# Moving the PSUM copies of tiles 1 to 14 from ScalarE to VectorE, and more single-row fetches to ScalarE and SyncE

## What is computed

```python
x0 = emb[ids].reshape(ids.shape[0], -1)
x = x0
for i in range(cross_w.shape[0]):            # 3 cross layers
    s = x @ cross_w[i]
    x = x0 * s[:, None] + cross_b[i] + x
h = relu(x0 @ w1 + b1)                       # 1664 -> 1024
h = relu(h @ w2 + b2)                        # 1024 -> 512
h = relu(h @ w3 + b3)                        # 512 -> 256
logit = concatenate([x, h], axis=1) @ out_w + out_b
return sigmoid(logit)
```

## Time and profile before

| | us |
|---|---|
| median of 3 runs (529.99 to 531.2) | 531.18 |
| the profiled execution | 530.56 |
| its span on the core | 528.8 |
| so outside the span | 1.76 |
| TensorE matmuls busy | 480.8 (91%) |
| VectorE busy | 186.4 (35%) |
| ScalarE busy (without issuing DMAs) | 84.7 (16%) |
| GpSimd busy | 379.6 (72%) |

### The profile page before, as it was taken

How to read it: one execution, slowest core, us unless ns; L and a number is a source line. 1 busy time by engine, 2 the same in 40 slices (tenths; PEclk the granted TensorE clock), 3 DMA queues, 4 the chain that set the end, 5 groups by cost and what they waited for, 6 DMA issues and landing times.

```text
span 528.8 us, 11324 instructions
## 1 busy us (share of the span) xinstructions
PE 480.8 (91%) x2912; PEld 442.2 (84%) x2912; DVE 186.4 (35%) x391; ACT 84.7 (16%) x159; POOL 379.6 (72%) x407
## 2 busy tenths in 40 slices
PE   2699899899999989899898989999899898999997
PEld 1399698898989889798887988888898888989996
DVE  5766414232142423224242321424232142423325
ACT  4642111111011111102011110101111010101111
POOL 5777776777777777777777777777777777777720
PEclk9999999999999999999999999999999999999999
DMA  7971111111111111111111111111111111111100
GB/s 234 387 263 29 28 29 27 28 29 27 29 29 29 28 28 30 29 29 29 27 29 26 30 27 30 26 30 29 26 30 25 30 27 28 27 28 28 28 10 2
DMA packets 19700, 24.90 MB, mean 47 GB/s; under 512 B 9305, under 2 KB 10292, under 8 KB 19636
## 3 DMA queue, kind: packets, MB, share of 16 engines
q0 software_dynamic: 12800, 13.13, 11.2%
q1 hardware_dynamic: 4770, 10.74, 5.7%
q10 hardware_dynamic: 2066, 0.31, 0.3%
HBM read 24.41 MB, written 0.01 MB: 46 GB/s over the span
## 4 chain that ended last, share of the span: by engine, by line
PE 55%; POOL 14%; issue 10%; ACTq 9%; DMA 5%; DVE 4%; ACT 3%; POOLq 0%; DVEq 0%
PE l_bank L717 41%; POOL x_raw L347 14%; ACTq L387 8%; DMA x_raw<-in_L_rec_emb,idx 4%; PE x_bank L717 4%; PE x_bank L729 4%; PE h_bank L771 3%; ACT xT_hi L400 2%; DVE x_raw L516 2%; ACTq L384 1%; PE l_bank L802 1%; DVE xT_lo L523 1%; PE h_bank L741 1%; DVE h2T_lo L528 1%; ACT h2T_hi L411 1%
## 5 line engine op out<-in xcount | busy, mean ns | idle before, releaser
L347 POOL DMA_INDIRECT x_raw<-in_L_rec_emb,idx x400 | 378.8, 947 | 125.5 <-issue 107.7
L717 PE MATMUL l_bank<-w_hi,xT_hi 128*128 128x342 f32 (+1 forms) x624 | 144.9, 333 | 3.5 <-DVE xT_lo L523 3.3
L717 PE MATMUL l_bank<-w_lo,xT_hi 128*128 128x342 f32 (+1 forms) x624 | 137.9, 321 | 0.0
L717 PE MATMUL l_bank<-w_hi,xT_lo 128*128 128x342 f32 (+1 forms) x624 | 137.7, 321 | 0.0
L717 PEld LDWEIGHTS l_bank<-w_hi,xT_hi 128*128 128x128 f32 x624 | 104.0, 191 | 7.9 <-DVE xT_lo L523 5.6
L717 PEld LDWEIGHTS l_bank<-w_lo,xT_hi 128*128 128x128 f32 x624 | 106.8, 191 | 0.0
L717 PEld LDWEIGHTS l_bank<-w_hi,xT_lo 128*128 128x128 f32 x624 | 106.3, 190 | 0.0
L523 DVE TENSOR_TENSOR xT_lo<-x_bank,xT_hi 128x512 fp32r<-128x512 f32 (+1 forms) x66 | 38.2, 578 | 158.5 <-ACT xT_hi L400 158.5
L400 ACT ACTIVATE xT_hi<-x_bank 128x512 fp32r<-128x512 f32 (+1 forms) x66 | 33.5, 507 | 270.3 <-PE x_bank L729 220.4
L729 PE MATMUL x_bank<-identity,x_raw 128*128 128x128 f32 x208 | 34.7, 279 | 27.0 <-DVE x_raw L516 27.0
L729 PEld LDWEIGHTS x_bank<-identity,x_raw 128*128 128x128 f32 x208 | 25.0, 142 | 36.7 <-issue 31.0
(11 more groups left out here) (94 smaller groups left out, 296.5 us busy)
## 6 DMA issues: line engine op xcount, KB each, us to landing
ids<-in_L_rec_emb SPq DMA_DIRECT2D x1152, 0.2 KB
ids<-in_L_rec_emb ACTq DMA_DIRECT2D x896, 0.2 KB
w_raw<-in_L_rec_w SPq DMA_DIRECT2D x18, 512.0 KB, 15.0
x_raw<-in_L_rec_emb,idx POOLq DMA_INDIRECT x400, 2.4
b_rows<-in_L_rec_b SPq DMA_DIRECT2D x1, 512.0 KB
b_rows<-in_L_rec_b SPq DMA_DIRECT2D x1, 256.0 KB
ids<-in_r_ids SPq DMA_DIRECT2D x1, 208.0 KB, 2.7
b_rows<-in_L_rec_b SPq DMA_DIRECT2D x1, 128.0 KB
```

The costliest lines, as they stand in the source:

```text
L347: pool.indirect_dma_start(out=dst, out_offset=None, in_=emb, in_offset=rows).then_inc(landed, 16)
L717: done = pe.matmul(bank[:, 0:b - a], x[:, k, :], w[:, k, a:b], start=(k == 0 and n == 0), stop=(k == last_k and n == 2))
```

## The change

1. The fields fetched row by row are those of chunk 10, the last chunk of group 2 (before: of chunk 12, in group 3). So the places are waited for by `make_whole` of group 2. SyncE fetches field 21 of tiles 2 to 14 (13 tiles, before 9). The rows of the biases, five DMAs, are issued by ScalarE in the first step, ahead of `x_hi(0, 1)`, and no longer by SyncE.
2. ScalarE fetches field 20 of ten tiles (3, 4, 5, 6, 8, 9, 10, 11, 13, 14; before seven tiles).
3. From tile 1 to 14 VectorE makes the copies `x_hi`, `h1_hi` and `h2_hi`, each right ahead of the subtraction that reads it.
4. ScalarE's step t is then: wait until group 0 of tile t is transposed, place what belongs to tile t, and fetch 104 rows in four shares of 26.
5. In tile 15 nothing is fetched row by row; ScalarE makes its copies there and in tile 0 as before.

`LAST_GROUPS` and the pacing of GpSimd stay. GpSimd now fetches chunk 12 of every tile and leaves out of chunk 10 what the others fetch: 393 gathers where it issued 400, that is 25 fields of tiles 2, 7 and 12, 24 of the other tiles from 3 to 14, and 26 of tiles 0, 1 and 15.

```diff
-    SP_TILES = [2, 4, 6, 8, 9, 10, 12, 14, 15]
+    SP_TILES = list(range(2, TILES - 1))
-    SP_FIELD = F - 2
+    SP_FIELD = GROUPS[2][-1] * FPK + 1
-    ACT_TILES = [3, 5, 7, 9, 11, 13, 15]
-    ACT_FIELD = F - 1
+    ACT_TILES = [3, 4, 5, 6, 8, 9, 10, 11, 13, 14]
+    ACT_FIELD = GROUPS[2][-1] * FPK
-    ACT_SHARES = [8, 12, 4, 16, 12, 12]
+    ACT_SHARES = [26, 26, 26, 26]
...
-            sync.wait_ge(idx_ready, 3)
-            for rows, vec in ((b1_rows, b1), (b2_rows, b2), (b3_rows, b3), (out_w_rows, out_w[D:D + N3, 0]), (out_b_rows, out_b)):
-                sync.dma_start(rows[:, :], vec.rearrange("(o n) -> o n", o=1).broadcast_to([P, rows.shape[1]])).then_inc(rows_loaded, 16)
...
             def fetch(share):
+                while share > 0 and fetched[0] < P * len(ACT_TILES):
+                    j, p = fetched[0] // P, fetched[0] % P
+                    if p == 0 and j >= ACT_BUFS:
+                        act.wait_ge(act_placed, j - ACT_BUFS + 1)
+                    row, rows = AT_ROWS.index((ACT_FIELD, ACT_TILES[j])), min(share, P - p)
+                    regs = [act.alloc_register(f"act_row{j}_{p + i}") for i in range(rows)]
+                    act.load(regs, at_bytes[row:row + 1, p:p + rows])
+                    for i, reg in enumerate(regs):
...
+                    fetched[0] += rows
+                    share -= rows
...
             def step(t):
-                fetch(ACT_SHARES[0])
-                x_hi(t, 0)
-                fetch(ACT_SHARES[1])
-                h2_hi(t - 1)
-                fetch(ACT_SHARES[2])
-                x_hi(t, 1)
-                fetch(ACT_SHARES[3])
-                x_hi(t, 2)
+                if t in SP_TILES or t in ACT_TILES:
+                    act.wait_ge(x_transposed, NG * t + 1)
                 if t in SP_TILES:
                     sp_place(t)
                 if t in ACT_TILES:
                     act_place(t)
-                fetch(ACT_SHARES[4])
-                x_hi(t, 3)
-                fetch(ACT_SHARES[5])
-                h1_hi(t)
+                for share in ACT_SHARES:
+                    fetch(share)
...
+            def x_hi(t, g):
+                dve.wait_ge(x_transposed, NG * t + g + 1)
+                ks = groups(t)[g]
+                dve.tensor_copy(xT_hi[:, ks[0]:ks[-1] + 1, :].rearrange("p k b -> p (k b)"),
+                                x_bank[g % 2][:, 0:len(ks) * P]).then_inc(xT_hi_ready, 1)
...
+            def step(t):
+                make_whole(t, 0)
+                x_hi(t, 0)
+                x_lo(t, 0)
+                l2_out(t - 1)
+                make_whole(t, 1)
+                x_hi(t, 1)
+                x_lo(t, 1)
+                h2_hi(t - 1)
+                h2_lo(t - 1)
+                for g in range(2, NG):
+                    make_whole(t, g)
+                    x_hi(t, g)
+                    x_lo(t, g)
+                l1_out(t)
+                dots_out(t)
+                h1_lo(t)
+                l3_out(t - 1)
```

More of the change, by code:

```diff
@@ L44, in dcn_ranker_kernel @@
     LOW_BITS = 2 ** (H.bit_length() - 1) - 1
-    SP_TILES = [2, 4, 6, 8, 9, 10, 12, 14, 15]
+    SP_TILES = list(range(2, TILES - 1))
     SP_REGS = 32
-    SP_FIELD = F - 2
+    SP_FIELD = GROUPS[2][-1] * FPK + 1
     SP_BUFS = 4
-    assert SP_FIELD // FPK in GROUPS[-1] and SP_FIELD // FPK in LAST_GROUPS[3]
-    ACT_TILES = [3, 5, 7, 9, 11, 13, 15]
-    ACT_FIELD = F - 1
+    ACT_TILES = [3, 4, 5, 6, 8, 9, 10, 11, 13, 14]
+    ACT_FIELD = GROUPS[2][-1] * FPK
     ACT_BUFS = 2
-    ACT_SHARES = [8, 12, 4, 16, 12, 12]
-    assert ACT_FIELD // FPK in GROUPS[-1] and all(
-        sum(ACT_SHARES) * (t - 1) >= P * (j + 1) for j, t in enumerate(ACT_TILES)) and P % sum(ACT_SHARES) == 0
+    ACT_SHARES = [26, 26, 26, 26]
+    assert all(sum(ACT_SHARES) * (t - 1) >= P * (j + 1) for j, t in enumerate(ACT_TILES))
+    ONE_RUNS = [(SP_FIELD, range(2, TILES - 1)), (ACT_FIELD, range(3, 7)), (ACT_FIELD, range(8, 12)), (ACT_FIELD, range(13, 15))]
+    AT_ROWS = [(f, t) for f, tiles in ONE_RUNS for t in tiles]
+    assert sorted(AT_ROWS) == sorted([(SP_FIELD, t) for t in SP_TILES] + [(ACT_FIELD, t) for t in ACT_TILES])
     ROW = E * 4
@@ L154, in dcn_ranker_kernel @@
         at_bytes = sb("at_bytes", [ONE_BY_ONE, P], I32)
-        at_row = {t: i for i, t in enumerate([t for t in SP_TILES if t % 2 == 0] + [t for t in SP_TILES if t % 2])}
         VR = (2 * CROSS + 1) * K1
@@ L291, in _ @@
                     regs = [sync.alloc_register(f"sp_row{i}_{p + j}") for j in range(SP_REGS)]
-                    sync.load(regs, at_bytes[at_row[t]:at_row[t] + 1, p:p + SP_REGS])
+                    row = AT_ROWS.index((SP_FIELD, t))
+                    sync.load(regs, at_bytes[row:row + 1, p:p + SP_REGS])
                     for j, reg in enumerate(regs):
@@ L367, in split_hi, with load_rows @@
                 act.activation(hi, raw, ACT.Copy).then_inc(hi_split, 1)
+            def load_rows():
+                act.wait_ge(idx_ready, 3)
+                for rows, vec in ((b1_rows, b1), (b2_rows, b2), (b3_rows, b3), (out_w_rows, out_w[D:D + N3, 0]), (out_b_rows, out_b)):
+                    act.dma_start(rows[:, :], vec.rearrange("(o n) -> o n", o=1).broadcast_to([P, rows.shape[1]])).then_inc(rows_loaded, 16)
             def sp_place(t):
@@ L377, in fetch @@
             def fetch(share):
[L379 to L389, removed]
+                while share > 0 and fetched[0] < P * len(ACT_TILES):
[6 more added lines that the diff above has]
+                    for i, reg in enumerate(regs):
+                        at = act.snap(reg, donate=True, min_val=0, max_val=(2 * H - 1) * ROW)
+                        act.dma_start(act_rows[j % ACT_BUFS][p + i:p + i + 1, :].bitcast(U8),
+                                      emb_bytes[:, bass.DynSlice(at, ROW)], bounds_check="skip_entire_dma").then_inc(act_landed[j % ACT_BUFS], 16)
+                    fetched[0] += rows
+                    share -= rows
             def act_place(t):
@@ L431, in first_step @@
                             cross_hi()
+                    if g == 1:
+                        load_rows()
                     x_hi(0, g)
@@ L447, in step @@
                     act_place(t)
-                fetch(ACT_SHARES[4])
-                x_hi(t, 3)
-                fetch(ACT_SHARES[5])
-                h1_hi(t)
+                for share in ACT_SHARES:
+                    fetch(share)
             def last_step(t):
+                assert t not in SP_TILES and t not in ACT_TILES
                 x_hi(t, 0)
                 h2_hi(t - 1)
[L456 to L462, removed]
+                for g in range(1, len(LAST_GROUPS)):
                     x_hi(t, g)
@@ L518, in make_whole, with relu_hi, h1_hi, h2_hi @@
                                     end_bank.rearrange("p (o e) -> p o e", o=1).broadcast_to([P, n, E])).then_inc(x_whole, 1)
+            def x_hi(t, g):
[3 more added lines that the diff above has]
+                                x_bank[g % 2][:, 0:len(ks) * P]).then_inc(xT_hi_ready, 1)
+            def relu_hi(bank, cols, hi, done):
+                dve.tensor_scalar(hi, bank[:, 0:cols], 0.0, None, ALU.max).then_inc(done, 1)
+            def h1_hi(t, half):
+                dve.wait_ge(h1_transposed, 2 * t + half + 1)
+                relu_hi(h_bank[half], HB * P, h1T_hi[:, half * HB:(half + 1) * HB, :].rearrange("p k b -> p (k b)"), h1T_hi_ready)
+            def h2_hi(t):
+                dve.wait_ge(h2_transposed, t + 1)
+                relu_hi(h_bank[0], K3 * P, h2T_hi[:, :, :].rearrange("p k b -> p (k b)"), h2T_hi_ready)
             def x_lo(t, g):
@@ L568, in h1_lo @@
                 for half in range(2):
+                    if t > 0:
+                        h1_hi(t, half)
                     dve.wait_ge(h1T_hi_ready, 2 * t + half + 1)
@@ L635, in first_step, with last_step @@
                 h1_lo(0)
-            def begin(t):
+            def step(t):
[16 more added lines that the diff above has]
+                l3_out(t - 1)
+            def last_step(t):
                 make_whole(t, 0)
@@ L643, in begin @@
                 x_lo(t, 1)
[L645 to L656, removed]
                 l3_out(t - 1)
@@ L692, in _ @@
             copied = 0
[L693 to L697, removed]
+            for field, tiles in ONE_RUNS:
+                a, b, every = tiles[0] * F + field, tiles[-1] * F + field, tiles.step
                 dve.scalar_tensor_tensor(out=sp_cols[:, copied:copied + len(tiles)], in0=past[:, a:b + 1:every * F], scalar=float(H),
@@ L909, in _ @@
             pe.wait_ge(cross_ready, 1)
-            pe.wait_ge(sp_cols_ready, 3)
+            pe.wait_ge(sp_cols_ready, len(ONE_RUNS))
             pe.transpose(x_bank[1][0:ONE_BY_ONE, 0:P], sp_cols, identity[:, :]).then_inc(sp_cols_transposed, 1)
```

## The result

The changed kernel takes 603.48 us (median of 4 runs, 603.12 to 603.91) against 531.19: 1.1367 times the time before, 95% interval 1.1347 to 1.1386. The forecast was 651.5 with a range of 636 to 672: slower was right, and the place of the loss too, but the size was 48 us too large, outside the range.

What follows compares the result with a forecast made beforehand. ScalarE's queue was to bound the changed kernel from tile 3, where TensorE with some GpSimd did before. Span 528.8 + 119.5 - 0.7 + 2 = 649.6, with 1.76 outside 651.4; forecast 651.5, bounds 638 to 672, stated range 636 to 672.

Steps and rivals of the forecast that it cites:

- The gate: On ScalarE's queue, places wait behind 104 rows; VectorE's patch and TensorE's group 2 transposes follow, 42 us a tile from tile 3.
- Bound by ScalarE's queue though ScalarE is idle: ScalarE's queue, where issuing DMAs doesn't count as busy, sets the pace: 42.0 us a step against TensorE's 30.55.
- The row's price: Each single-row DMA on ScalarE's queue costs 0.325 us, 0.234 of it the least recorded DMA time.
- rival 1: ScalarE's rows get cheap without copies between them, 0.195 us each; step 28.5 us, time 524.4, faster; chance 0.06.
- The load's price: ScalarE's load of n registers ahead of a share costs 0.35 + 0.053n us; bound on this term 6 us.
- TensorE's own pace: TensorE, not held up by others, would take 30.55 us a tile.
- The slow restart: TensorE's matmuls run slow after a wait; only after tile 13's does it reach the end: +2 us, 0 to +9.
- rival 3: TensorE stays slow all tile long after its waits, some 52 us or more a tile; time some 780; chance 0.04.
- From group 2 of tile 13 to the end: The kernel's tail: group 2 of tile 13 at 562.6 us, span ending at 649.6.
- SyncE's share in the price of ScalarE's rows: On ScalarE's queue, more rows issued by SyncE should not make ScalarE's rows dearer than 0.234 us.
- GpSimd, the bias rows, VectorE's load: GpSimd's relief counts 0, bias rows moved to ScalarE 0 (0 to +1), VectorE's 48 to 70 us of copies hidden, 0.
- rival 2: ScalarE's loads run beside the DMAs ahead of them; step 34.8 us, time 564; chance 0.05.

Runs made afterwards that it cites:

- c4: Kernel before with only the copies moved to VectorE and bias rows to ScalarE, old fields, 64 rows a step in shares of 16: 528.57 us, ratio 0.9968.
- d2: Kernel before with one constant changed, ScalarE fetching field 22 instead of field 25 row by row: 529.25 us, ratio 0.9984.
- d1: Changed kernel with shares 28, 24, 28, 24, but ScalarE fetching field 25 and SyncE field 24 instead of 20 and 21: 660.06 us, ratio 1.2455.
- b3: Changed kernel with shares of 28, 24, 28, 24 rows for four of 26: 516.34 us, ratio 0.9728 to the kernel before.
- b1: Kernel before with only the five bias-row DMAs moved from SyncE to ScalarE: 530.45 us, ratio 0.9996.

## Why the prediction was right in kind and wrong in size

- **The gate** (places behind 104 rows, the patch behind the places, TensorE behind the patch, from tile 3 on): right, as the timelines of tile 13 show. From tile 2 on the tiles are 37 to 40 us apart, and the patch of tile 13 waits 7.8 us for the place, where 42 and some 11 were forecast.
- **Bound by ScalarE's queue though ScalarE is idle**: right; 59% of the chain.
- **The row's price: the step that failed first.** 0.325 us a row was read from rows that said so without exception, and it was a price of field 25's ids, not of a row. SyncE's 0.195 stood beside it as the mean of a field whose rows are mostly dropped (field 24, 137 of 1152 in the table), and I gave it to rival 1 with the wrong condition ("no copies between them", which c4 and d2 exclude) and 0.06. The diff moved the field and the reference has the ids' bounds; both were at hand. d2 and d1 show it from either side. In the sum it was 150 us too much.
- **The load's price: the second.** The line 0.35 + 0.053n was fitted to aligned loads only the earlier trace rows, the shares of 26 aren't. 103 us too little; b3, which aligns them, is 87 us faster, and then GpSimd holds it. The bound on this term was 6 us, which took the spread of the points for what the line could miss; the rows gave no load at an address like the new ones.
- **Rival 1** was half true: the rows are that cheap. Its 524 would have needed the aligned loads; b3, which has both, gives 516.3. The 8 us below it are the next point.
- **TensorE's own pace** was put at 30.55 us a tile. In the kernel after, between tile 13 and 14, it is 28.90 (529.73 to 558.63 below), and as much in b3. The 30.55 holds waits of 1.7 us a tile: in the three tiles from 84 to 175.6 us, at the same pace, TensorE waits 3.3 us for the patch of group 1 and 1.8 for the low part of group 2. Both stand behind copies of ScalarE that stand behind a fetch, as this stretch of before's chain shows (12 rows end at 125.62). The forecast took one wait of 0.7 us out of rows 12 for tile 14, and had no term for the patch.

```profile
PE x_bank L729 <- DVE x_raw L516: 3.3, 3, 1.2
PE l_bank L717 <- DVE xT_lo L523: 1.8, 3, 0.6
```
```profile
125.39 0.23 ACTq L387
125.62 0.05 issue
125.67 0.61 ACT h2T_hi L411
126.30 0.69 DVE h2T_lo L528
126.99 0.50 DVE x_raw L516
```

The chain of the kernel after, from the transposes of tile 13 on:

```profile
515.16 1.08 PE x_bank L745 x4
516.24 7.60 PE l_bank L733 x36
...
529.73 1.15 PE h_bank L787 x8
...
558.63 1.15 PE h_bank L787 x8
```

- **The slow restart**: right in size, by luck in part. 36 matmuls take 7.60 us after the wait and 5.70 otherwise, and the transposes 1.08 for 0.63: 2.35 us for the 2 forecast. But the price came from matmuls that were slow at a granted clock of 1.00, so not from the clock; here the clock is low:

```profile
172.00:174.00 2.00, 2.00 (x9) 2.00 (x8) 1.35 (x3) 0.00 (x0) 0.65 (x1) 0.50 0.00 0
178.00:186.00 8.00, 8.00 (x54) 7.83 (x52) 2.17 (x5) 0.00 (x0) 5.87 (x8) 1.00 0.11 26
```

(stretch, its length, busy time of TensorE, its weight loads, VectorE, ScalarE, GpSimd, then the granted clock, the share of the DMA engines and GB/s). TensorE stands still until 171.49 here. Just behind, from 172 to 174, the clock is at its lower level, 0.50 or 1.2 GHz; from 178 on it is at 1.00 or 2.4 GHz. So rival 3 (slow all tile long) is out, and in tiles 3 to 12 the loss hides in the next wait, as said.

- **From group 2 of tile 13 to the end**: 601.3 - 515.2 = 86.1 us, forecast 87.0.
- **SyncE's share in the price of ScalarE's rows** was put at none. The medians bear that out, but "the trace disagrees" says too much, for single records show something: in the kernel before, without the first rows behind the loads, 21 of the 382 rows during which SyncE had a row on record took more than 0.245 us, and 1 of the 430 others; in d1 33 of 697 and 3 of 524. On the mean that is 0.002 us a row, nothing in the sum.
- **GpSimd, the bias rows, VectorE's load**: as forecast; GpSimd's relief pays nothing here, VectorE is busy for 59 us more (48 to 70 forecast), b1 shows no change.
- **Two slips in the sums** that changed nothing: the terms of the upper bound add up to about 674, not 672, and rival 2's 564 leaves out the terms -0.7 and +2.

What the change might have been: with shares of 28 and 24, one line, it is 2.7% faster than the kernel before.

## What to carry to other kernels

A price read from a trace belongs to the data as much as to the instruction: before carrying it over, ask which of its inputs the change moves (here the column of ids, and whether a bounds check drops them). A straight line through sizes says nothing of a size outside their common property; look for what the measured ones share (all multiples of four) and the new one doesn't. And two wrong terms can partly cancel: 48 us off was 150 and 103.

## What the runs showed of the hardware

- A single-row DMA of 256 bytes takes ScalarE's queue 0.235 us as a record, and 0.090 where the bounds check drops it; SyncE 0.238 and 0.073. The first row in the table behind each load of registers takes ScalarE 0.47 us (all 84 loads of the kernel before, 0.466 to 0.532); a share's 0.14 us "on top" in the forecast is that. A dropped one makes no packets on the queue, a row in the table two.
- A load of registers from SBUF costs, by estimate from its times, about 0.35 us and 0.2 us a read: four registers at an address that is a multiple of 16 bytes, one at an address 8 bytes off it (26 registers: 2.13 and 5.8 us). Addresses 4 or 12 bytes off weren't tried.
- Behind a wait of TensorE of 6.92 us three l1 matmuls took 1.06 us at 516.90 and 0.63 at 521.31; behind one of 7.37 us the granted clock of the stretch from 172 to 174 us was 0.50, and 1.00 from 178 on.
